# A fused four-layer kernel, first phase: group-level VectorE work dealt out over more units, half of the gathers placed one unit sooner, sorted rows loaded in six transfers

## The chip, the cores and the metric

One core of one Trainium2 chip. The metric is the device time of one execution in microseconds, the median over several runs. The engines are PE (TensorE), DVE (VectorE), ACT (ScalarE), POOL (GpSimd) and SP (SyncE, which here only issues DMAs). A line number such as L741 is a line of the kernel before.

## The reference, cut to what matters

Four layers, each a cross attention and a feed-forward part with a residual; batch 32, 128 rows, width 128, all float32. The first phase of the kernel computes layer 0 and the attention of layer 1:

```python
x = x + L0_xattn(layernorm(x), ctx, ctx, mask0, wo, bo)      # 16 heads of 8, softmax, relu(ctx @ wo.T + wo_b)
x = x + L0_ffn(layernorm(x), Wr, br, W1, b1, W2, b2)         # 8 experts, top 2, hidden 512
x = x + L1_xattn(layernorm(x), ctx, ctx, mask1, ...)         # 16 heads of 8, softmax
# L0_ffn, for each row: logits = x @ Wr + br; the two largest, softmax of them as gates;
# out = sum over the two experts e of gate[e] * (relu(x @ W1[e] + b1[e]) @ W2[e] + b2[e])
```

Every expert is applied only to the rows that chose it: the rows are sorted by expert in DRAM, and gathered back afterwards.

## The kernel before, in words

The batch is cut into 8 groups of 4 batch entries (512 rows). The first phase runs 16 streams one after another: stream j = 0 to 7 is the attention of layer 0 for group j, stream 8 to 15 the attention of layer 1 for group j - 8. Each stream has 8 units (u = 0 to 7, 8 heads of one batch entry each), so there are 128 units, n = 8 j + u, and 16 more steps for what trails. In unit n PE computes scores (L851), DVE adds or clips with the mask (L582, L586) and reduces to the negative row maximum (L1206), ACT applies the exponential (L981); one unit later PE transposes the result (L865) and ACT and DVE copy it out (L973, L976 or L1213), two units later PE multiplies by the values (L883), then turns the result back (L890), and DVE normalises it (L1184, L1188). Each engine runs its own instructions in order; a function work(place, n) of each engine holds what is done once per group, hung on a unit and a place in it. DVE has places 0 to 3; place 3 is the end of its unit, behind the maximum.

Work done once per group, and where it stands before the change (stream j runs, u is the unit in it):

- front: LayerNorm of the next layer 0 stream's rows. DVE statistics at u = 0, place 3 (L1091 and L1092; the instructions are L329, L333, L336), the power on POOL at u = 1 (L340), the scaling on DVE at u = 1 (L345), transposes on PE at u = 3 (L730), copy qT on ACT (L929), queries on DVE at u = 4 (L1057).
- router of the group two streams back: comparisons on DVE at u = 0, place 3 (router_dve), gates at u = 2, place 3 (router_gates_dve), turned by PE at u = 4 (L810) and copied by DVE at u = 4 (L1159).
- ranking, once for each pair of groups, at u = 2, place 3: rank_dve gives the sorted place of each row (the index, last line L436), rank_tiles_dve the expert of each of 23 tiles (L443 to L447), rank_gates_dve the two gates of each row (L456 to L460).
- scatter: POOL writes the rows to sorted_in in DRAM by 16 indirect DMAs, four per unit at u = 4 to 7 (L1035).
- load: SP reads all 23 sorted tiles (128 rows of 128) back to SBUF, one unit before the pair's first tile unit (load_sorted, L689). It waits for the scatters and, from the second pair on, for the turns of the pair before.
- tiles: four pairs of groups, their tiles in units 34 to 50, 51 to 67, 68 to 84 and 85 to 101. For each pair there are 6 turns (PE transposes a quad of 4 tiles, L741; ACT copies, L904), 23 hidden products (L747; relu on ACT L911 or DVE L1067), 23 output products (L755), 6 copies back (L919) and stores to sorted_out (L709). The first tile unit has turn 0 and three hidden tiles; the second turn stands in the next unit, the later ones three units apart. SP loads the weights of a tile four tiles ahead (L682); it waits for the output product that frees the buffer.
- gathers: for layer 1's stream of group g POOL gathers 4 + 4 blocks of rows from sorted_out at the start of u = 0 of the stream before (L1011), and DVE adds them with their gates (combine, L1076 and L1081) at u = 3, place 3, just ahead of the late statistics (L1112; L329 again). Then follow power (L340), scaling at u = 4 (L345), transposes (L730), query product.
- last_ln: DVE statistics at u = 7, place 3, power on POOL at u = 7.

PE's bank 6 serves all of this group-level work in turn; each use waits until the use before has been read (function aux).

## Time and profile before

| what | value |
|---|---|
| median of 3 runs | 2143.19 us (2140.99 to 2145.85) |
| the profiled execution's own time | 2141.56 us |
| its span | 2139.8 us |
| mean granted TensorE clock | 0.955 |
| busy over the span: PE, DVE, ACT, POOL | 87%, 70%, 61%, 29% |
| first phase, from unit 0's maximum to the last unit's | 45.4 to 839.1 us |

The span is from the first to the last instruction of one profiled execution. The granted clock is the share of full TensorE speed that the chip allowed. In a row of the trace in order of time the first number is the start in us from the span's start, the second the duration in us, then engine, line, operation, what is written <- what is read, shape and count; in brackets the idle time of the engine just before it and what ended that.

### The profile page before, as it was taken

What the parts mean: (1) busy time and instruction counts of PE and PEld (TensorE: products, weight loads), DVE (VectorE), ACT (ScalarE), POOL (GpSimd) and SP (SyncE); (2) the same over time, 40 slices, a digit from 0 to 9 for tenths busy, and PEclk for the clock granted to TensorE, in tenths of its full rate; (3) what the DMA queues carried; (4) which work ended last, traced back from release to release, by engine and by line L of the source; (5) the groups of instructions that cost most, each with busy time, mean ns of one, the idle gap of its engine ahead of it and who ended that gap; (6) DMA issues with size and microseconds to landing.
All of it is one profiled execution on the core that took longest, in us unless ns stands there. A gap on an engine that the chain in (4) does not pass through costs nothing.

```text
span 2139.8 us, 49953 instructions
## 1 busy us (share of the span) xinstructions
PE 1861.7 (87%) x17669; PEld 1515.4 (71%) x17669; DVE 1488.4 (70%) x3873; ACT 1303.8 (61%) x4466; POOL 617.2 (29%) x610
## 2 busy tenths in 40 slices
PE   3987998989989988657888889999999988898878
PEld 2776887778878776545666677777877876676665
DVE  5887786878878887666776675766757565655556
ACT  1976665556666777536676766666666654544432
POOL 0003031131522220024343333254452523333321
PEclk9998999999999999858899989999999999999999
DMA  8013354354544100310000011222222223232351
GB/s 242 17 31 102 108 151 141 118 163 128 156 146 144 50 21 6 130 46 20 29 6 15 6 43 38 87 81 85 73 73 69 82 82 95 72 99 72 109 146 49
DMA packets 119637, 178.44 MB, mean 83 GB/s; under 512 B 9824, under 2 KB 77728, under 8 KB 119136
## 3 DMA queue, kind: packets, MB, share of 16 engines
q1 hardware_dynamic: 111712, 159.51, 24.6%
q0 software_dynamic: 7680, 15.74, 2.4%
q8 instruction: 144, 2.36, 0.5%
q14 instruction: 101, 0.83, 0.1%
HBM read 141.26 MB, written 33.95 MB: 82 GB/s over the span
## 4 chain that ended last, share of the span: by engine, by line
PE 37%; DVE 9%; ACT 6%; issue 4%; POOL 1%; DMA 0%; DVEq 0%; ACTq 0%; SPq 0%
PE ps L1659 5%; PE ps L1944 5%; PE ps L1892 3%; PE ps L1697 3%; PE ps L1885 3%; ACT pb L2093 3%; PE ps L1681 2%; PE ps L1866 2%; PE ps L1688 2%; PE ps L1670 2%; DVE nm L2472 2%; PE ps L1707 1%; PE ps L1715 1%; PE ps L1914 1%; PE ps L1858 1%
## 5 line engine op out<-in xcount | busy, mean ns | idle before, releaser
L2093 ACT ACTIVATE pb<-ps,nm 128x128 f32<-128x128 f32 x1024 | 364.1, 379 | 196.0 <-DVE nm L2472 195.9
L2141 POOL TENSOR_TENSOR pb<-pb,rcs 128x512 f32<-128x512 f32 x256 | 268.5, 1050 | 663.0 <-DVE rcs L2480 662.2
L981 ACT ACTIVATE pb<-pb,nm 128x128 f32<-128x128 f32 x1024 | 313.2, 394 | 31.7 <-DVE nm L1206 29.9
L2497 DVE COPY pt<-ps 128x512 f32<-128x512 f32 x128 | 88.3, 690 | 198.2 <-PE ps L1944 198.1
L2093 ACT ACTIVATION_READ_ACCUMULATOR pb<-ps,nm 128x1 f32 x1024 | 222.5, 217 | 0.0
L2472 DVE TENSOR_REDUCE nm<-ps 128x8 f32<-128x1024 f32 x128 | 155.9, 1218 | 63.5 <-PE ps L1892 40.3
L1944 PE MATMUL ps<-w,pb 128*128 128x128 f32 x1024 | 167.4, 288 | 22.5 <-ACT pt L2101 10.3
L1206 DVE TENSOR_REDUCE nm<-pb 128x8 f32<-128x1024 f32 x128 | 156.2, 1220 | 4.4
L1944 PEld LDWEIGHTS ps<-w,pb 128*128 128x128 f32 x1024 | 121.4, 147 | 46.6 <-ACT pt L2101 20.1
L865 PE MATMUL ps<-w,pb 128*128 128x128 f32 x1024 | 145.9, 287 | 5.4 <-ACT pb L981 5.2
L2101 ACT ACTIVATE pt<-ps 128x512 f32<-128x512 f32 x128 | 77.0, 602 | 91.0 <-PE ps L1944 90.9
L865 PEld LDWEIGHTS ps<-w,pb 128*128 128x128 f32 x1024 | 125.1, 149 | 9.7 <-issue 7.5
L1659 PE MATMUL ps<-hT,big 128*128 128x128 f32 x840 | 116.8, 283 | 13.8 <-DVE hT L2243 13.4
L1659 PEld LDWEIGHTS ps<-hT,big 128*128 128x128 f32 x840 | 105.0, 194 | 33.5 <-DVE hT L2243 21.0
L973 ACT ACTIVATE pt<-ps 128x512 f32<-128x512 f32 x128 | 76.4, 597 | 65.5 <-PE ps L865 64.4
L747 PE MATMUL ps<-h_all,big 128*128 128x128 f32 x736 | 104.3, 287 | 12.2 <-DVE hT L1067 5.7
L747 PEld LDWEIGHTS ps<-h_all,big 128*128 128x128 f32 x736 | 93.3, 198 | 19.0 <-DVE hT L1067 7.5
L966 ACT ACTIVATE ou<-ps 128x256 f32<-128x256 f32 x128 | 48.4, 378 | 92.9 <-DVE h_all L1188 47.0
L755 PE MATMUL ps<-big,hT 128*128 128x128 f32 x736 | 101.7, 282 | 0.0
L1975 ACT ACTIVATE hT<-ps 128x256 f32<-128x256 f32 x133 | 50.9, 383 | 75.7 <-PE ps L1659 75.0
L755 PEld LDWEIGHTS ps<-big,hT 128*128 128x128 f32 x736 | 92.1, 196 | 5.5 <-issue 2.2
L1681 PE MATMUL ps<-h_all,big 128*128 128x512 f32 x128 | 71.5, 640 | 26.3 <-ACT h_all L2014 26.3
(379 smaller groups left out, 4407.0 us busy)
## 6 DMA issues: line engine op xcount, KB each, us to landing
big<-in_we SPq DMA_DIRECT2D x92, 514.0 KB, 3.7
big<-in_we SPq DMA_DIRECT2D x109, 384.0 KB, 3.1
sorted_out<-big SPq DMA_DIRECT2D x27, 256.0 KB
big<-sorted_in SPq DMA_DIRECT2D x7, 960.0 KB, 5.7
sorted_in<-big SPq DMA_DIRECT2D x4, 1472.0 KB, 12.2
hidden<-h_all SPq DMA_DIRECT2D x7, 512.0 KB, 2.9
h_all<-hidden SPq DMA_DIRECT2D x7, 512.0 KB, 3.8
sorted_out<-h_all SPq DMA_DIRECT2D x14, 256.0 KB
```

What stands on the lines that cost most here:

```text
L747: m = pe.matmul(ps[:, 5, c * P:(c + 1) * P], w1_0[:, k % NWS, c, :], xsT0[:, (NQ0 * g + t // 4) % 4, (t % 4) * P:(t % 4 + 1) * P], start=T ...
L755: m = pe.matmul(ps[:, 7, (t % 4) * D:(t % 4 + 1) * D], hT[:, k % 4, c * P:(c + 1) * P], w2_0[:, k % NWS, c, :], start=(c == 0), stop=(c == ...
L865: m = pe.transpose(ps[:, 2 + k // 4, (k % 4) * S:(k % 4 + 1) * S], pb[:, p % 2, k * S:(k + 1) * S], ident)
L981: m = a.activation(pb[:, n % 2, k * S:(k + 1) * S], pb[:, n % 2, k * S:(k + 1) * S], ACT.Exp, bias=nm[:, n % 2, k:k + 1])
L1206: v.tensor_reduce(nm[:, n % 2, :], buf, AX, ALU.max, negate=True).then_inc(s["maxed"], 1)
L1659: m = pe.matmul(ps[:, bank, (2 * half + c) * P:(2 * half + c + 1) * P], weights[:, half, c, :], rows_T, start=True, stop=True)
L1681: pe.matmul(ps[:, BANK_A, :], q3_w[:, c, :], yT3[g % 2], start=True, stop=True)\
L1944: m = pe.transpose(ps[:, BANK_T, k * S:(k + 1) * S], pb[:, p % 2, (4 * half + k) * S:(4 * half + k + 1) * S], ident)
L2093: m = a.activation(pb[:, n % 2, e * S:(e + 1) * S], ps[:, score_bank(n) + half, k * S:(k + 1) * S], ACT.Exp, bias=nm[:, n % 2, e:e + 1], a ...
L2141: g_.tensor_tensor(p4, p4, r4.unsqueeze(2).to_broadcast([P, 4, S]), ALU.mult).then_inc(n2["p_normed"], 1)
L2472: v.tensor_reduce(nm[:, n % 2, :], ps[:, bank:bank + 2, :].rearrange("p a (j k) -> p (a j) k", k=S), AX, ALU.max, negate=True).then_inc(n2 ...
L2497: v.tensor_copy(pt[:, p % 2, 4 * S:8 * S], ps[:, BANK_T, :]).then_inc(n2["p_lo"], 1)
```

## The change

- The front statistics move from u = 0 to u = 7, place 3, of the unit before; those of group 1 stay in unit 0.
- combine moves from u = 3 to u = 2, place 3; the late statistics stay.
- rank_tiles_dve and rank_gates_dve move from u = 2 to u = 3, place 3.
- Of the eight gathers of a group the first four, with their waits, stand at the end of u = 7 in POOL's program, the other four where all stood.
- load_sorted issues six transfers, one per quad. Transfers 3 to 5 wait until the transfer three places before has landed; three semaphores take turns. A turn waits for its own quad.
- The semaphore group_loaded, which nothing used, goes.

```diff
--- before.py
+++ after.py
@@ -247,7 +247,6 @@
             counted.append(s)
             return s
 
-        group_loaded = isem("group_loaded")
         loaded = [isem(f"loaded_{n}") for n in range(2)]
         v_pool = isem("v_pool")
         v_dve = isem("v_dve")
@@ -301,6 +300,7 @@
                                                    "row_psum", "row_added", "down_read", "q2_psum", "q2_col", "v2_psum",
                                                    "bias_bo2", "bias_bos", "bias_bout3"]))
         weights_loaded = [isem(f"weights_loaded_{n}") for n in range(NWS)]
+        sorted_quads = [isem(f"sorted_quad_{q}") for q in range(3)]
         moe = {name: isem(f"moe_{name}") for name in
                ["sel", "rank", "index", "tiles", "scattered", "gathered", "sorted_loaded", "xT_psum", "xT", "turned_back",
                 "stored", "first_added", "b2_added", "logits", "logit_row", "shifted", "gate_exp", "gates", "gateT_psum", "gateT", "hid_psum",
@@ -684,10 +684,15 @@
 
                 def load_sorted(g):
                     sp.wait_ge(moe["scattered"], 16 * 2 * PB * (g + 1))
-                    if g:
-                        sp.wait_ge(moe["xT_psum"], NQ0 * g)
-                    sp.dma_start(xs0[:, :, :], xs_d[g].rearrange("(t p) d -> p t d", p=P))\
-                        .then_inc(moe["sorted_loaded"], 16)
+                    for q in range(NQ0):
+                        first, end = quad(q, NT0)
+                        if g:
+                            sp.wait_ge(moe["xT_psum"], NQ0 * (g - 1) + q + 1)
+                        if q >= 3:
+                            sp.wait_ge(sorted_quads[q % 3], 16 * (2 * g + 1))
+                        sp.dma_start(xs0[:, first:end, :],
+                                     xs_d[g].rearrange("(t p) d -> p t d", p=P)[:, first:end, :])\
+                            .then_inc(sorted_quads[q % 3], 16)
 
                 loads(0)
                 for n in range(NUN):
@@ -736,7 +741,7 @@
                         pe.wait_ge(*before0[(g, kind, t)])
                     if kind == "turn":
                         first, end = quad(t, NT0)
-                        pe.wait_ge(moe["sorted_loaded"], 16 * (g + 1))
+                        pe.wait_ge(sorted_quads[t % 3], 16 * (2 * g + t // 3 + 1))
                         for i in range(first, end):
                             m = pe.transpose(ps[:, 5, (i - first) * P:(i - first + 1) * P], xs0[:, i, :], ident)
                         m.then_inc(moe["xT_psum"], 1)
@@ -996,21 +1001,20 @@
                     g_.tensor_copy(vas[j % 2][:, :, :, 0:DH].rearrange("p b h d -> p (b h) d"),
                                    ctx[:, :, :].rearrange("p b (h d) -> p (b h) d", h=H)).then_inc(v_pool, 1)
 
+                def gather(g, ks):
+                    for k in ks:
+                        e = k // G * PB + g % 2 * G + k % G
+                        g_.indirect_dma_start(yg0[:, k, :], None, ys_d[g // 2],
+                                              bass.IndirectOffsetOnAxis(ap=sort0[g // 2].idx[:, e:e + 1], axis=0))\
+                            .then_inc(moe["gathered"], 16)
+
                 pow_(front, 1)
                 values(0, 0)
                 for n in range(NUN + 2 * NU):
                     j, u = divmod(n, NU)
                     layer, g = stream(j + 1)
                     if layer == 1 and u == 0:
-                        g_.wait_ge(moe["stored"], 16 * NQ0 * (g // 2 + 1))
-                        if g:
-                            g_.wait_ge(moe["gathered"], 16 * 2 * G * g)
-                            g_.wait_ge(moe["combined"], g)
-                        for k in range(2 * G):
-                            e = k // G * PB + g % 2 * G + k % G
-                            g_.indirect_dma_start(yg0[:, k, :], None, ys_d[g // 2],
-                                                  bass.IndirectOffsetOnAxis(ap=sort0[g // 2].idx[:, e:e + 1], axis=0))\
-                                .then_inc(moe["gathered"], 16)
+                        gather(g, range(G, 2 * G))
                     if layer == 0 and u == 1:
                         pow_(front, g + 1)
                     if layer == 0 and u == 2:
@@ -1034,6 +1038,13 @@
                         for k in range(4 * (u - 4), 4 * (u - 3)):
                             g_.indirect_dma_start(xs_d[p], bass.IndirectOffsetOnAxis(ap=sort0[p].idx[:, k:k + 1], axis=0),
                                                   expert_ys[(2 * p + k % PB // G) % 3][:, k % G, :], None).then_inc(moe["scattered"], 16)
+                    layer, g = stream(j + 2)
+                    if layer == 1 and u == 7:
+                        g_.wait_ge(moe["stored"], 16 * NQ0 * (g // 2 + 1))
+                        if g:
+                            g_.wait_ge(moe["gathered"], 16 * 2 * G * g)
+                            g_.wait_ge(moe["combined"], g)
+                        gather(g, range(G))
                 g_.wait_ge(moe["gathered"], 16 * 2 * G * NG)
                 g_.wait_ge(moe["scattered"], 16 * 2 * G * NG)
 
@@ -1088,8 +1099,10 @@
                     j, u = divmod(n, NU)
                     here = (place, u)
                     layer, g = stream(j + 1)
-                    if layer == 0 and here == (3, 0):
-                        stats(front, g, g + 1)
+                    if n == 0 and place == 3:
+                        stats(front, 1, 2)
+                    if stream(j + 2)[0] == 0 and here == (3, 7):
+                        stats(front, g + 1, g + 2)
                     if layer == 0 and here == (3, 1):
                         v.wait_ge(front.yT_psum, g)
                         apply(front, g, g + 1)
@@ -1107,8 +1120,9 @@
                                         ps[:, 6, :].rearrange("p (b h d) -> p b h d", b=G, h=H),
                                         R("bv1").rearrange("p (h d) -> p h d", h=H).unsqueeze(1)
                                         .to_broadcast([P, G, H, DH]), ALU.add).then_inc(v_dve, 1)
+                    if layer == 1 and here == (3, 2):
+                        combine(g)
                     if layer == 1 and here == (3, 3):
-                        combine(g)
                         stats(late, g, g + 1)
                     if layer == 1 and here == (3, 4):
                         v.wait_ge(late.yT_psum, g)
@@ -1152,8 +1166,9 @@
                         router_gates_dve(v, link, picked0[g % 2], gates0[g % 2], g + 1)
                         if g % 2:
                             rank_dve(v, link, sort0[g // 2], sel_z[:, 0:PB, :], 6, g // 2 + 1)
-                            rank_tiles_dve(v, link, sort0[g // 2])
-                            rank_gates_dve(v, link, sort0[g // 2], gates[:, :, :])
+                    if layer == 0 and g % 2 and here == (3, 3):
+                        rank_tiles_dve(v, link, sort0[g // 2])
+                        rank_gates_dve(v, link, sort0[g // 2], gates[:, :, :])
                     if layer == 0 and here == (1, 4):
                         v.wait_ge(moe["gateT_psum"], g + 1)
                         v.tensor_copy(gateT, ps[0:E0, 6, :]).then_inc(moe["gateT"], 1)
```

## Rows read from the trace of the kernel before

**Rows 1.** Stretch 33.5 to 845 us: busy PE, PEld, DVE, ACT, POOL; PEclk, DMA, GB/s.
```profile
33.50:845.00 811.50, 727.50 (x7884) 622.02 (x7884) 647.31 (x1547) 553.54 (x1634) 173.13 (x175) 0.96 0.34 101
```

**Rows 2.** Waits of PE, 100 to 845 us: total us, times, longest.
```profile
PE ps L741 <- DMA big<-sorted_in: 18.5, 4, 6.8
...
PE ps L810 <- ACT qT L929: 6.2, 4, 2.9
```

**Rows 3.** PE in order of time: the four waiting turns, and transposes behind one.
```profile
215.19 1.12 PE L741 MATMUL ps<-w,big 128*128 128x128 f32 x4 [6.75 <-DMA big<-sorted_in]
...
337.54 1.09 PE L741 MATMUL ps<-w,big 128*128 128x128 f32 x4 [3.98 <-DMA big<-sorted_in]
338.42 1.92 PE L865 MATMUL ps<-w,pb 128*128 128x128 f32 x8
...
349.16 1.04 PE L865 MATMUL ps<-w,pb 128*128 128x128 f32 x8
...
468.45 1.09 PE L741 MATMUL ps<-w,big 128*128 128x128 f32 x4 [4.46 <-DMA big<-sorted_in]
...
599.83 1.09 PE L741 MATMUL ps<-w,big 128*128 128x128 f32 x4 [3.31 <-DMA big<-sorted_in]
```

**Rows 4.** SP's queue in order of time, around the loads of pairs 0 and 1.
```profile
207.32 0.72 SPq L689 DMA_DIRECT2D big<-sorted_in  x1
...
328.64 0.74 SPq L689 DMA_DIRECT2D big<-sorted_in  x1
330.17 3.60 SPq L682 DMA_DIRECT2D big<-in_we  x1
```

**Rows 5.** Issue to landing in us: L689 (1472 KB), L682 (514 KB), 960 KB loads.
```profile
DMA to landing us min/median/max: 7.8/9.3/10.4
...
DMA to landing us min/median/max: 3.3/3.7/9.4
...
big<-sorted_in SPq DMA_DIRECT2D x7, 960.0 KB, 5.7
```

**Rows 6.** DVE, then PE, in order of time, around unit 16.
```profile
109.82 0.21 DVE L1184 RECIPROCAL rc<-ps 128x8 f32<-128x8 f32 x1 [0.87 <-PE ps L890]
...
113.37 0.86 DVE L329 BATCH_NORM_STATS2 st_front<-x_all 128x6 f32<-128x128 f32 x4
...
114.76 0.18 DVE L356 TENSOR_TENSOR lg<-ps,rows 128x32 f32<-128x32 f32 x1
...
118.56 0.62 PE L883 MATMUL ps<-pt,h_all 128*9 128x128 f32 x16 [1.40 <-ACT ou L966]
```

**Rows 7.** DVE, then PE, in order of time, units 26 to 28.
```profile
168.56 0.16 DVE L443 TENSOR_TENSOR cmp_a<-cmp_a 128x8 f32<-128x8 f32 x1
...
170.72 0.21 DVE L1184 RECIPROCAL rc<-ps 128x8 f32<-128x8 f32 x1
...
176.67 1.01 PE L810 MATMUL ps<-w,gates 128*8 128x128 f32 x4 [2.88 <-ACT qT L929]
```

**Rows 8.** POOL in order of time: pair 0's last scatter, group 6's last gather.
```profile
204.76 0.96 POOL L1035 DMA_INDIRECT sorted_in<-hT,big  x1 [0.30 <-issue]
...
740.43 0.95 POOL L1011 DMA_INDIRECT big<-sorted_out,big  x1 [0.30 <-issue]
```

**Rows 9.** DVE in order of time, unit 68.
```profile
468.28 0.67 DVE L1159 COPY big<-ps 8x512 f32<-8x512 f32 x1
```

**Rows 10.** PE at 652 and 710 us, DVE in units 106 and 107, in order of time.
```profile
652.45 0.66 PE L741 MATMUL ps<-w,big 128*128 128x128 f32 x4 [0.84 <-DVE hT L1067]
...
710.55 1.08 PE L730 MATMUL ps<-w,y 128*128 128x128 f32 x4 [1.59 <-DVE y L345]
...
738.92 1.22 DVE L1206 TENSOR_REDUCE nm<-pb 128x8 f32<-128x1024 f32 x1
...
744.56 1.13 DVE L1076 SCALAR_TENSOR_TENSOR x_all<-big,x_all 128x128 f32<-128x128 f32 x4
...
746.90 0.87 DVE L329 BATCH_NORM_STATS2 st_late<-x_all 128x6 f32<-128x128 f32 x4
```

## The prediction

> **What bounds the kernel now.** I read four views, in this order. First the busy time of the stretch that the change touches: the 128 units of the first phase. PE is busy 727.5 of 811.5 us there, DVE 647.3, ACT 553.5, at a mean granted clock of 0.96 [rows 1]. So PE leads and DVE is close behind; what can be won is PE's 84 us of waits and its time at the lower clock. I count units from 0 by the row-maximum reductions (L1206). Second, the waits of PE. The largest group, 18.5 us in four waits, is the turn of the sorted rows (L741) waiting for the load from sorted_in [rows 2]. Third, PE in order of time: the four waits are 6.75, 3.98, 4.46 and 3.31 us, at 215, 338, 468 and 600 us [rows 3], one for each pair of groups, in units 33/34, 51, 68 and 85. The reader should also see what follows such a wait: the eight transposes of L865 take 1.92 us, and 1.04 us a unit later [rows 3]. That is one half and full clock (1.2 and 2.4 GHz). Fourth, DVE around its heavy units, to see whether its bursts reach PE; they do in some (below).
>
> **Sorted rows in six transfers.** Now one load of 1472 KB lands 7.8, 9.3 or 10.4 us (least, median, most) after its issue [rows 5], and the first turn waits for all of it although it reads four of 23 tiles, 256 KB. No row has a 256 KB part of it. From below: 960 KB of the same pattern land in 5.7 us [rows 5], so (7.8 - 5.7) / 512 KB is 0.0041 us per KB, and 256 KB come to 5.7 - 704 x 0.0041 = 2.8 us, an estimate. From above: a 514 KB weight load, 3.7 us median and 9.4 at worst [rows 5]. I take 3.5, near the first two, and keep 9.4 for a rival.
> - Pair 0: issued at 207.32 [rows 4], first quad at 210.8 instead of the turn at 215.19: 4.4 us.
> - Pair 1: issued at 328.64 [rows 4], quad at 332.1. PE was ready at 337.54 - 3.98 = 333.56, so all 3.98 go.
> - Pair 2: landing within 10.4 us of issue means issue at 458 or later, quad by 461.6 or little after; PE was ready at 463.99. But the next use of the auxiliary bank, L786, waits for DVE's copy L1159, and DVE is in an unbroken row of work until that copy ends at 468.28 + 0.67 = 468.95 [rows 9]. The turn and L865 took 2.6 us from 468.45 to L786 at 471.0. So only 471.0 - 468.95 = 2.1 us go, the rest becomes a wait for DVE.
> - Pair 3: PE was ready at 599.83 - 3.31 = 596.5; all 3.3 go.
> - Clock: behind pair 1's wait L865 costs 1.92 - 1.04 = 0.9 us too much [rows 3]; the turn ahead of it (half as many matmuls) and the eight matmuls behind it run at the same clock, by the same ratio 0.4 and 0.8: 2.1 us. Of this I take half at pairs 1 and 3, 2.1 in all, since smaller waits stay.
>
> Together 4.4 + 4.0 + 2.1 + 3.3 + 2.1 = **15.9 us**. On SP's queue the five more issues (some 0.4 us each) and the waits of transfers four to six for the landing of one to three stand ahead of the next weight load and of the store of a finished quad. The sixth can be issued about 3.5 + 2 = 5.5 us after the first. That costs nothing as long as this queue is no more blocked than now: the weight load behind the big transfer already sits 3.6 us and more in its issue [rows 4], so that SP is free only at about 334.5, 5.9 us after 328.64. The third hidden tile needs that weight some 8 us later. The later quads are read one to four units (7 us each) later. Cost taken: 0.
>
> The Trainium skill (DMA: Bandwidth & Descriptors, section "Anatomy of one DMA — SWDGE (gpsimd) path") fits a transfer by 2.0 us plus bytes over 436 GB/s, which speaks against splitting: six times 2.0 us fixed instead of once. By it the first quad would land in 2.6 us and the whole load in 5.5; the trace disagrees on the latter, 7.8 at least [rows 5]. With the page's value the pair 0 term would be 5.3 instead of 4.4.
>
> **LayerNorm statistics of the front stream one unit sooner.** They take 114.76 - 113.37 = 1.4 us of DVE [rows 6] and now share the unit with the router's comparisons. In unit 16 this makes PE wait 1.40 us for the context (L883) behind ACT behind DVE [rows 6]. In the unit before, DVE waits 0.87 us before its reciprocal [rows 6] and again before the mask, so the 1.4 us find room. Gain 1.4 in unit 16 and 1.4 in 24, the same pattern. Unit 32 gains nothing: there all waits for pair 0's scatters on POOL, which run back to back to 204.76 + 0.96 [rows 8]. Units 8, 40 and 48: 0.3 in all, since PE is nearly without wait there. **3.1 us.**
>
> **Tile table and gates of the ranking one unit later.** 170.72 - 168.56 = 2.2 us of DVE [rows 7], four times. In unit 26 they delay the maximum, so the exponentials, so ACT's copy of qT, for which PE's L810 waits 2.88 us [rows 7]. I take 1.7 of the 2.2. Pair 1 has the same wait inside the total of 6.2 us in four [rows 2]; less is left there because expert matmuls fill PE: 1.0. In pairs 2 and 3 the combine moves the other way between the same two units, so DVE's sum is unchanged: 0. **2.7 us.** SP's first weight loads wait for this table; it comes no later in time than it is needed, as they are used 8 units on.
>
> **Gathers.** POOL's order does not change. The four gathers that now stand at the end of unit u = 7 are directly followed by the other four at the start of u = 0, with nothing between them, and the waits ahead of them are the same. Gain and cost 0; queued behind them is only POOL's next power.
>
> **Combine one unit sooner.** 746.90 - 744.56 = 2.3 us of DVE [rows 10] leave the unit of the late statistics. Groups 0 to 3: 0. Group 4: PE's wait of 0.84 us for the hidden tile [rows 10] goes: 0.8. Group 5: the wait of 1.59 us for y goes (L730) [rows 10], and with it 0.9 of the 2 us that the low clock costs behind such a wait. Against it: combine now needs its gathers one unit sooner, and the gathers don't come sooner. The landing time is not in the trace; the nearest row is the scatter's, 207.32 - 205.72 = 1.6 us from the end of its last issue to SP's load [rows 4, 8]. Group 6: the last gather ends its issue at 741.38 [rows 8], lands at 743.0; DVE reaches the combine at 738.92 + 1.22 = 740.1 [rows 10] and waits 2.9 us. It ends at 745.3; normalising and mask 1.6, maximum 1.1, bias 0.6 follow, so the late statistics start at 748.7 instead of 746.90 [rows 10]: 1.8 us later. Group 7, the same with 1.1 us less wait: 0.8. Sum 0.8 + 1.6 + 0.9 - 2.6 = **0.7 us**.
>
> **Sum.** 15.9 + 3.1 + 2.7 + 0.7 = 22.4 us. The profiled execution took 2141.56 us (span 2139.8), 1.6 us under the median of the runs, 2143.19; the gain is taken off either. From the median: 2120.8 us.
>
> **Rivals.**
> - *More than the sum.* The clock comes back wholly after all stalls (2 us more), the bursts of DVE behind L883, L810 and L730 vanish earlier, the first quad lands in 2.8 us and the gathers before DVE asks: some 10 us more, 2111. For it: DVE has no wait in most heavy units. Against: moved work is not removed.
> - *First quad late.* It shares the engines with weight loads that need up to 9.4 us [rows 5]; at 9 us the four waits stay, and only 6.5 us are won: 2136.7.
> - *SP blocked.* If a quad takes 5 us, transfer six goes out after 11 us and the weight for the third hidden tile comes 3 to 4 us late, at three pairs: 10 us back, 2131. For it: its issue is already blocked 3.6 us [rows 4]. Against: the blockage is part of today's time too.
> - *Slower: DVE waits for gathers.* The combine stands in order on DVE, ahead of the next mask and maximum. With gathers that land x us later than 1.6, groups 6 and 7 lose x each, groups 3 to 5 too beyond about 3 us of slack. That reaches the other 25 us at x about 7, a landing of 8 to 9 us; beyond, at 10, the kernel takes 2147. Only the large load shows such landings [rows 5], and a gather moves 64 KB.
> - *Not what it says.* The gathers' part, certain by the order on POOL; it is in the sum.
>
> **Chances.** Forecast (gain 15 to 28) 0.62; more 0.12; first quad late 0.11; SP blocked 0.09; slower 0.04; a trade that leaves nothing 0.02. The range takes the first four, 2111 to 2134. A change under 0.2%, 4.3 us, cannot be told from none in this kernel. Faster by more 0.91, within 0.05, slower 0.04.
>
> **What would show it.** L741 waits for sorted_in under 3 us in sum, only at pair 0; transfers about 3.5 us to landing; units 16 and 24 about 1.4 us shorter; L810 waits under 1 us at unit 28; eight gathers still 1.27 us apart in one row; a new wait of DVE at the first combine line near units 106 and 114. Wrong if L741 still waits 3 us and more at pairs 1 to 3, if L747 waits for weights behind the quads, or if DVE's wait for gathers shows in groups 3 to 5.

## The result and the profile after

The changed kernel takes 2115.11 us (median of 4 runs, 2109.54 to 2117.64), the kernel before 2144.52 in the runs timed with it (2140.99 to 2152.38). The ratio is 0.9863, 95% interval 0.9838 to 0.9888: 1.4% faster. The forecast, 2120.8 us or a ratio of 0.9896, was right in its direction and its range (2111 to 2134), and too small in its size: the gain between the two medians is 29.4 us, 22.4 were forecast, and 29.4 lies a little above the band of 15 to 28 that the prediction gave to its forecast, in that of the rival "more than the sum". The profiled execution took 2117.64 us with a span of 2115.9, 23.9 us under that of before.

The code is longer, so behind the sorted load the line numbers of the changed kernel are 4 to 15 higher, save those of the gathers: L741, L747, L786 and L865 became L746, L752, L791 and L870; L883 became L888 and L810 L815; L1076 and L1206 became L1087 and L1221; the gathers are L1007, the sorted load L693.

First the stretch of the 128 units, which answers to [rows 1] (busy PE, PEld, DVE, ACT, POOL; granted clock, DMA share, GB/s):

```profile
33.50:819.50 786.00, 721.78 (x7884) 615.33 (x7884) 646.60 (x1546) 553.15 (x1634) 172.91 (x175) 0.97 0.35 104
```

The stretch is 25.5 us shorter with the same 7884 matmuls. DVE does as much as before (646.6 us against 647.3); PE's busy time fell by 6 us, as fewer of its matmuls ran at half clock (granted 0.97 instead of 0.96); the other 20 us are waits of PE that are gone. Next the waits of PE in this stretch, the view of [rows 2] (total us, times, longest):

```profile
PE ps L791 <- DVE big L1174: 7.3, 4, 3.0
PE ps L752 <- DMA big<-in_we: 6.9, 4, 2.6
...
PE ps L815 <- ACT qT L934: 3.9, 3, 1.6
PE ps L888 <- ACT ou L971: 3.8, 4, 2.1
PE ps L746 <- DMA big<-sorted_in: 2.6, 1, 2.6
```

The wait of the turns for the sorted rows was 18.5 us in four and is 2.6 in one, at pair 0. A new one stands in its place: the hidden products wait 6.9 us for weights. In the kernel before these stood at 1.9 us, and the waits for the context (L883, now L888) at 8.9:

```profile
PE ps L883 <- ACT ou L966: 8.9, 10, 1.5
...
PE ps L747 <- DMA big<-in_we: 1.9, 2, 1.1
```

PE in order of time shows where (compare [rows 3]):

```profile
202.25 1.12 PE L746 MATMUL ps<-w,big 128*128 128x128 f32 x4 [2.64 <-DMA big<-sorted_in]
...
318.16 1.16 PE L856 MATMUL ps<-ctxT,qm 32*128 32x128 f32 x16
...
326.94 2.05 PE L752 MATMUL ps<-h_all,big 128*128 128x128 f32 x8 [2.25 <-DMA big<-in_we]
328.92 2.08 PE L856 MATMUL ps<-ctxT,qm 32*128 32x128 f32 x16
...
450.46 1.09 PE L791 MATMUL ps<-w,h_all 128*128 128x128 f32 x4 [2.82 <-DVE big L1174]
...
581.18 1.13 PE L752 MATMUL ps<-h_all,big 128*128 128x128 f32 x8 [2.59 <-DMA big<-in_we]
582.24 1.78 PE L856 MATMUL ps<-ctxT,qm 32*128 32x128 f32 x16
```

These are pair 0, the third hidden tile of pairs 1 and 3, and at pair 2 the wait for DVE's copy that the prediction named. Behind the weight waits PE runs at half clock again: the sixteen matmuls of L856 took 1.16 us ahead of the wait and take 2.08 and 1.78 behind it. SP's queue at pair 1 answers to [rows 4]:

```profile
314.54 6.46 SPq L693 DMA_DIRECT2D big<-sorted_in  x6
321.77 1.47 SPq L682 DMA_DIRECT2D big<-in_we  x2
```

The six issues hold SP for 6.5 us, and the next weight load leaves 7.2 us after the first of them. The times from issue to landing of the 24 transfers (20 of 256 KB, four of 192 KB), which answer to [rows 5]:

```profile
DMA to landing us min/median/max: 2.8/3.5/5.7
```

Last, DVE in order of time in units 106 and 107, the view of [rows 10]:

```profile
711.00 1.22 DVE L1221 TENSOR_REDUCE nm<-pb 128x8 f32<-128x1024 f32 x1
715.02 1.14 DVE L1087 SCALAR_TENSOR_TENSOR x_all<-big,x_all 128x128 f32<-128x128 f32 x4 [2.80 <-DMA big<-sorted_out,big]
...
720.73 0.86 DVE L329 BATCH_NORM_STATS2 st_late<-x_all 128x6 f32<-128x128 f32 x4
```

Combine waits 2.80 us for its gathers; at group 7 it waits 1.85. It waits at group 3 too, in unit 82, 0.45 us:

```profile
559.51 1.14 DVE L1087 SCALAR_TENSOR_TENSOR x_all<-big,x_all 128x128 f32<-128x128 f32 x4 [0.45 <-DMA big<-sorted_out,big]
```

### The profile page after: what moved, and what is told of

The parts are those of the page before. It is cut to its first block, busy times and chain, and to the rows that moved or that the text cites. A ratio compares the mean times of both kernels' runs of the same rounds, so it can differ in the third digit from the quotient of the medians.

```text
span 2115.9 us, 49981 instructions
## 1 busy us (share of the span) xinstructions
PE 1859.6 (88%) x17665; PEld 1511.9 (71%) x17669; DVE 1486.2 (70%) x3873; ACT 1302.6 (62%) x4466; POOL 616.5 (29%) x610
## 4 chain that ended last, share of the span: by engine, by line
PE 38%; DVE 9%; ACT 6%; issue 4%; POOL 1%; DMA 0%; DVEq 0%; ACTq 0%; SPq 0%
PE ps L1674 5%; PE ps L1959 5%; PE ps L1907 3%; PE ps L1712 3%; PE ps L1900 3%; ACT pb L2108 3%; PE ps L1696 3%; PE ps L1881 2%; PE ps L1703 2%; PE ps L1685 2%; PE ps L1722 1%; DVE nm L2487 1%; PE ps L1730 1%; PE ps L1929 1%; PE ps L1873 1%
## 5 line engine op out<-in xcount | busy, mean ns | idle before, releaser
L1221 DVE TENSOR_REDUCE nm<-pb 128x8 f32<-128x1024 f32 x128 | 156.2, 1220 | 4.4
L870 PE MATMUL ps<-w,pb 128*128 128x128 f32 x1024 | 141.8, 280 | 8.2 <-ACT pb L986 7.9
L870 PEld LDWEIGHTS ps<-w,pb 128*128 128x128 f32 x1024 | 120.4, 146 | 13.6 <-issue 10.6
L752 PE MATMUL ps<-h_all,big 128*128 128x128 f32 x736 | 103.9, 286 | 12.2 <-DMA big<-in_we 6.9
L752 PEld LDWEIGHTS ps<-h_all,big 128*128 128x128 f32 x736 | 92.9, 198 | 18.6 <-issue 9.1
```

The lines of the kernel that those rows point to most:

```text
L752: m = pe.matmul(ps[:, 5, c * P:(c + 1) * P], w1_0[:, k % NWS, c, :], xsT0[:, (NQ0 * g + t // 4) % 4, (t % 4) * P:(t % 4 + 1) * P], start=T ...
L870: m = pe.transpose(ps[:, 2 + k // 4, (k % 4) * S:(k % 4 + 1) * S], pb[:, p % 2, k * S:(k + 1) * S], ident)
L1221: v.tensor_reduce(nm[:, n % 2, :], buf, AX, ALU.max, negate=True).then_inc(s["maxed"], 1)
```

## The experiments

All edits concern the first phase, so I read each profile by one marker, the start of the last unit's maximum (839.1 us before, 813.5 changed), and by the lengths of short stretches of units, measured between starts of the maximum. A table of the lengths follows the last experiment. The experiments ran in three sessions, each on another chip. Six transfers alone, all but the six transfers and both repairs ran five or six times and have a ratio; each other kernel ran once, so of it only the profile is read, and no ratio is claimed.

**Six transfers alone.** Edit, to the kernel before (the unused group_loaded goes too):

```diff
-                    sp.dma_start(xs0[:, :, :], xs_d[g].rearrange("(t p) d -> p t d", p=P))\
-                        .then_inc(moe["sorted_loaded"], 16)
+                    for q in range(NQ0):
...
+                        if q >= 3:
+                            sp.wait_ge(sorted_quads[q % 3], 16 * (2 * g + 1))
+                        sp.dma_start(xs0[:, first:end, :],
+                                     xs_d[g].rearrange("(t p) d -> p t d", p=P)[:, first:end, :])\
+                            .then_inc(sorted_quads[q % 3], 16)
```

> The kernel before, with the sorted rows loaded in six transfers as the only edit (the unused semaphore group_loaded makes room for the new ones). Marker: the start of the last unit's maximum, 839.1 us before, 813.5 with the whole change. Theory 1, the sum of the prediction: the six transfers carry 15.9 us, so the marker is at 823 and the kernel takes 0.9926 of before. Theory 2, SP blocked: the issue of six transfers holds SP for 6 to 7 us, the third hidden tile of pairs 1 and 3 waits for its weights, 2 to 3 us each and the clock falls again, so only 11 to 12 us are left: marker at 827 to 828, ratio 0.995. In both the wait of the first turn for sorted_in stays only at pair 0, at 2 to 3 us. Theory 3, the waits were only covering DVE's backlog: under 6 us.

Ratio 0.9931 (0.9897 to 0.9965), which takes in both theories; marker 828.15, as theory 2 has it. Counted from unit 9 on, past units 0 to 8, which took 1.6 us longer here than before, 13.1 us were won: more than the 11 to 12 of theory 2, less than 15.9. The waits are those of theory 2, 2.28 us at pair 1 and 2.02 at pair 3. All waits of PE for DMAs in this kernel:

```profile
PE ps L752 <- DMA big<-in_we: 6.2, 4, 2.3
...
PE ps L746 <- DMA big<-sorted_in: 2.1, 1, 2.1
```

The weight waits at the third hidden tile are there with the six transfers alone, so they come from these. Units 85 and 86 together took 18.97 us, 21.90 before: of the 3.3 us wait and its clock, 2.9 us were won.

**All but the six transfers.** The same edit taken out of the changed kernel.

> The whole change without the six transfers (one load of 1472 KB again). Theory 1, the terms of the prediction for everything else: 3.1 + 2.7 + 0.7 = 6.5 us, marker at 832.6 (839.1 before), ratio 0.997. Theory 2, the steps read unit by unit from the changed kernel: units 16 and 24 1.3 each, units 26 to 28 4.2, units 90 to 101 about 4, units 106 and 114 minus 2.4: some 10 us, marker at 829. Theory 3, the parts need each other (the DVE work only matters once the load no longer stalls PE): under 3 us. If parts add up, the gains of this run and of the run with the six transfers alone give 25.6 together.

Ratio 0.9930 (0.9907 to 0.9954), marker 826.43, where the terms of the prediction gave 832.6. Counted from unit 9 to 127 the two halves won 13.1 and 12.5 us, 25.7 with rounding; the whole change won 25.1 in its first profile and 28.9 in another (below). So they add up as far as two profiles can tell, and theory 3 falls. The half without the transfers carried twice what I gave it (6.5). It won this although PE's waits for the one big load grew, from 18.5 us to 23.0: PE arrives earlier at a load that does not.

**A semaphore for each transfer.** In the changed kernel:

```diff
+        sorted_quads += [slot["hid_psum"], slot["hid"], slot["logits"]]
...
-                        if q >= 3:
-                            sp.wait_ge(sorted_quads[q % 3], 16 * (2 * g + 1))
...
-                            .then_inc(sorted_quads[q % 3], 16)
+                            .then_inc(sorted_quads[q], 16)
...
-                        pe.wait_ge(sorted_quads[t % 3], 16 * (2 * g + t // 3 + 1))
+                        pe.wait_ge(sorted_quads[t], 16 * (g + 1))
```

The three further semaphores are ones of the kernel's last phase; they are cleared between the phases.

> The changed kernel, each of the six transfers with a semaphore of its own, so that transfers four to six do not wait for the landing of one to three. Theory 1 (SP is held by these waits, and the new waits of L752 for weights, 2.25 us at pair 1 and 2.59 at pair 3, come from that): the six issues take 2.5 to 3 us instead of 6.5 to 7.1, the waits for weights at the third hidden tile vanish, the marker moves from 813.5 to 807 to 811. Theory 2 (the queue takes no more descriptors, as when the weight load sat 3.6 us in its issue behind the single load): the time moves into a long issue of transfer four to six or of the weight load, the waits stay, marker 813 to 814.

Marker 806.05. The weight waits at the third hidden tile are gone, but the six issues did not shrink to 3 us where other DMAs stood ahead. SP's queue of this kernel, pairs 0 and 1 (its code is two lines longer, so the weight loads are L684):

```profile
200.45 3.12 SPq L693 DMA_DIRECT2D big<-sorted_in  x6
...
315.07 5.33 SPq L693 DMA_DIRECT2D big<-sorted_in  x6
321.15 1.48 SPq L684 DMA_DIRECT2D big<-in_we  x2
```

And PE in order of time, the third hidden tile of pair 1:

```profile
326.46 1.16 PE L752 MATMUL ps<-h_all,big 128*128 128x128 f32 x8 [1.23 <-ACT hT L916]
```

Both theories are partly right. At pair 0 the issues take 3.1 us. At pair 1 they still take 5.3, one of them 1.87 us by itself: SP sits in the issues themselves, with no wait in the program. With both repairs (below) the same six took 4.0. The weight load leaves 6.1 us after the first transfer instead of 7.2. That 1.1 us is enough for the weights to arrive before ACT has emptied the bank, and the clock stays up: unit 51 takes 9.16 us at a granted clock of 1.00 instead of 11.68 at 0.76, units 85 and 86 16.59 at 1.00 instead of 20.73 at 0.84. One profile would be thin evidence, since the weight wait at pair 1 varies without any edit near it: over the eight profiles with six transfers and three semaphores it is 1.45 to 2.60 us, and in the two where it is shortest (gathers at u = 6 with 1.45, front statistics back with 1.51) unit 51 takes 9.35 and 9.41 us at full clock. But it is there in all eight, at pair 3 in seven of the eight, and at neither pair in the two profiles with six semaphores.

**Gathers really sooner.** In the changed kernel both halves of the gathers go to u = 6, ahead of the power of last_ln:

```diff
-                    if layer == 1 and u == 0:
-                        gather(g, range(G, 2 * G))
...
+                    layer, g = stream(j + 2)
+                    if layer == 1 and u == 6:
+                        g_.wait_ge(moe["stored"], 16 * NQ0 * (g // 2 + 1))
...
+                        gather(g, range(2 * G))
                     layer, g = stream(j - 1)
                     if layer is not None and u == (7 if layer else 5):
                         pow_(last_ln if layer else experts, g + 1)
...
-                    if layer == 1 and u == 7:
...
-                        gather(g, range(G))
```

> The changed kernel with all eight gathers and their waits one unit and a half sooner in POOL's program: at u = 6, ahead of the power of last_ln at u = 7. Theory 1 (the gathers start late because they stand behind POOL's wait for the last_ln statistics, and combine waits for them): combine's waits for sorted_out, 2.80, 1.85 and 0.45 us, vanish, and the marker moves 3 to 5 us, to 809 to 810.5. Theory 2 (the landing is late because of the DMA, not the order): the waits stay, marker at 813.5. Theory 3: POOL waits for the stores and holds up the power behind them, new waits of DVE for rs_last_ln, marker no better.

Marker 801.15, 12.4 us ahead of 813.5 where 3 to 5 were expected. Not all of that is the gathers': unit 51 and units 66 to 69 are 2.3 and 2.1 us shorter too, and 66 to 69 are as short in an unedited second profile (below). What the edit gave stands past unit 106: from there to the last unit's maximum 94.86 us, 102.51 and 99.52 in the two profiles of the changed kernel, 100.13 before, so 4.7 to 7.7 us. No wait of combine is left. POOL in order of time shows group 6's last gather ahead of the power, and in the changed kernel behind it the first, at 702.48:

```profile
696.73 0.95 POOL L1007 DMA_INDIRECT big<-sorted_out,big  x1 [0.30 <-issue]
697.70 1.05 POOL L340 TENSOR_TENSOR rs_last_ln<-ve_last_ln,half 128x4 f32<-128x4 f32 x1
```

```profile
701.28 1.02 POOL L340 TENSOR_TENSOR rs_last_ln<-ve_last_ln,half 128x4 f32<-128x4 f32 x1 [15.70 <-DVE ve_last_ln L336]
702.48 1.01 POOL L1007 DMA_INDIRECT big<-sorted_out,big  x1 [0.19 <-issue]
```

Units 106 to 109 take 17.68 us; 21.76 in the changed kernel, 20.13 before. In this profile the 2.80 us of waiting thus cost 4.1 us. Behind that wait of DVE, PE in the changed kernel waited too and fell to half clock:

```profile
718.37 0.62 PE L888 MATMUL ps<-pt,h_all 128*9 128x128 f32 x16 [2.13 <-ACT ou L971]
...
722.82 1.92 PE L870 MATMUL ps<-w,pb 128*128 128x128 f32 x8
```

It need not. In the second profile of the changed kernel DVE waits 2.73 us and PE 2.06 at the same places, and the clock stays up:

```profile
717.89 0.62 PE L888 MATMUL ps<-pt,h_all 128*9 128x128 f32 x16 [2.06 <-ACT ou L971]
...
718.82 1.16 PE L856 MATMUL ps<-kT,h_all 32*128 32x128 f32 x16
```

The stretch of units 106 to 109 as the windows show it (the clock is the last number but two), first profile, then second:

```profile
711.00:732.80 21.80, 19.66 (x201) 15.71 (x202) 16.48 (x39) 15.33 (x45) 4.20 (x4) 0.84 0.04 11
```

```profile
710.60:731.10 20.50, 17.00 (x200) 13.29 (x201) 16.27 (x39) 15.27 (x45) 4.22 (x4) 1.00 0.04 11
```

There the wait costs 2.8 us, 20.50 against 17.68: its own length and no more.

**Both repairs.** The two edits above together.

> The changed kernel with both edits that moved the marker: six semaphores for the six transfers, and all eight gathers at u = 6. Marker 813.5 with the change, 806.1 with the semaphores, 801.2 with the gathers. If the two act on different waits (weights at the third hidden tile; gathers at combine), they add up: marker at 793.7 to 795, ratio to before near 0.979. If both only shorten the same reserve of PE, under 3 us more than the gathers alone: marker above 798.

2100.75 us (2093.40 to 2107.45, 5 runs), ratio 0.9815 (0.9790 to 0.9840), marker 797.56. It is faster than the kernel before. By the two ratios to before it is some 0.5% under the changed one, but their intervals just overlap (up to 0.9840 and from 0.9838), so against the changed kernel the profile must carry the rest; against the gathers alone (one run, 2096.93 us) the times say nothing. In it unit 51 (9.16 us), units 85 and 86 (16.59) and units 106 to 109 (17.67) are each as short as in the better of the two single repairs, so the repairs act on different waits. The two single repairs put the marker 7.5 and 12.4 us ahead of 813.5, which would give 793.7 together. It is 4 us later, between the two answers expected (793.7 to 795; above 798). The single marker of the gathers held 2.3 us of unit 51, which the semaphores give too, and 2.1 of units 66 to 69, where one profile happened to keep the full clock; markers of one kernel differ by 3.4 us (below).

**Gathers together.** The gathers' part of the change undone: all eight at the start of u = 0.

> The changed kernel with the gathers' part undone: all eight gathers with their waits at the start of u = 0, as before the change. Theory 1 (the program order of POOL is the same, since nothing stands between the end of u = 7 and the start of u = 0): marker within 0.5 us of 813.5, gathers 1.27 us apart, the same waits of combine, 2.8, 1.9 and 0.5 us. Theory 2 (half of the gathers really start sooner in the changed kernel): combine waits longer by a unit, some 4 us at each of two groups, marker 818 and more.

Marker 810.83, combine waits 2.89, 1.64 and 0.67 us. Theory 1: this part of the change does nothing. The marker is even 2.7 us lower, outside the 0.5 us expected, though POOL's order is the same, and that had to be explained before any part could be read by its marker.

**The changed kernel once more.** No edit.

> The changed kernel itself, once more. If the profiles repeat apart from chance shifts, the marker lies between 810 and 815, combine waits 2.8, 1.9 and 0.5 us for its gathers, L752 waits about 2 us each for weights at pairs 1 and 3, and the first turn of pair 0 waits 2.6 us. If the marker comes out under 809 or over 817, the single-profile comparisons of the parts below 4 us say nothing by their marker.

Marker 810.12, span 2105.8. Combine waits 2.73, 1.74 and 0.77 us, L752 2.18 and 2.39 at pairs 1 and 3, the first turn 2.78, all close to what was expected. So the same kernel gives 813.5 and 810.1, and spans 10 us apart; the four timed runs of the changed kernel alone spread from 2107.8 to 2115.9 in span. The stretches in the table show that most repeat within 0.1 us and a few have two or more lengths, 1 to 2 us apart. Where they differ by more than 0.3 us, the granted clock differs. First and second profile: unit 20 takes 6.21 us at 1.00 and 7.86 at 0.78; units 26 to 28 17.54 at 0.90 and 16.78 at 1.00; 58 to 60 24.91 at 1.00 and 26.35 at 0.94; 66 to 69 35.34 at 0.90 and 33.22 at 1.00; 74 to 76 24.64 at 0.93 and 23.25 at 1.00; 106 to 109 21.76 at 0.84 and 20.50 at 1.00. Parts are read by stretches from here on. Behind the phase the time varies too: 1302.4 us from the marker to the end in one profile, 1295.7 in the other, 1300.7 before, 1294.0 to 1305.9 over all kernels here, none of which is edited there.

**Combine back at u = 3.**

```diff
-                    if layer == 1 and here == (3, 2):
-                        combine(g)
                     if layer == 1 and here == (3, 3):
+                        combine(g)
                         stats(late, g, g + 1)
```

> The changed kernel with combine back at u = 3 of every group. By the prediction's term the marker moves 0.7 us later, to 814.2. By the steps read unit by unit (units 82 to 84 gained 1.5, 90 to 92 1.5, 98 to 101 2.4; units 106 and 114 lost 1.6 and 0.8) it moves 3.0 us later, to 816.5. Rival: with the tile table now at u = 3 too, the burst of DVE in units 59 and 75 grows to 2.3 + 2.2 + 1.4 us at one place and PE waits more there: 818 and more. The waits of combine for gathers vanish in any case.

Marker 817.39. Units 82 to 84, 90 to 92 and 98 to 101 are back at 18.77, 19.57 and 26.05 us, the values of before; units 106 to 109 and 114 to 119 at 20.13 and 32.30, those of before too (21.76 and 33.05 in the first profile of the changed kernel, 20.50 and 31.33 in the second). And the rival shows at pair 2: units 58 to 60 take 28.73 us, more than ever, since combine, statistics and the tile table now stand in one place, and PE waits for the copy behind them:

```profile
393.94 1.09 PE L791 MATMUL ps<-w,o 128*128 128x128 f32 x4 [5.23 <-DVE big L1173]
```

In the changed kernel, second profile, the same wait is 2.99 us. So the two moves need each other at pair 2; alone, the move of the tile table would have cost some 2.3 us there (28.73 against 26.46 before), by this one profile.

**Tile table and gates back at u = 2.**

```diff
-                    if layer == 0 and g % 2 and here == (3, 3):
-                        rank_tiles_dve(v, link, sort0[g // 2])
-                        rank_gates_dve(v, link, sort0[g // 2], gates[:, :, :])
...
                             rank_dve(v, link, sort0[g // 2], sel_z[:, 0:PB, :], 6, g // 2 + 1)
+                            rank_tiles_dve(v, link, sort0[g // 2])
+                            rank_gates_dve(v, link, sort0[g // 2], gates[:, :, :])
```

> The changed kernel with the tile table and the gates of the ranking back at u = 2. By the prediction's term the marker moves 2.7 us later, to 816.2. By the steps of units 26 to 29 (4.2 us) and 42 to 45 (1.0 us) it moves 5.2 us later, to 818.7, with L815 waiting 2.9 us again at unit 28. Rival: at pairs 2 and 3 combine and the whole ranking then stand in one unit, 2.3 us more in a burst than ever before: another 2 us or more, marker above 820.5.

Marker 817.40. Units 26 to 28 take 19.86 us at a clock of 0.91, 2.3 more than the first profile with the move (0.90) and 3.1 more than the second (1.00), and L815 waits 2.9 us again; units 42 to 44 take 0.3 more, where I had 1.0. The rival at pairs 2 and 3 shows little: 27.03 us at pair 2 against 26.35 in the second profile (the first had 24.91, at full clock), and nothing at pair 3.

**Front statistics back at u = 0.**

```diff
-                    if n == 0 and place == 3:
-                        stats(front, 1, 2)
-                    if stream(j + 2)[0] == 0 and here == (3, 7):
-                        stats(front, g + 1, g + 2)
+                    if layer == 0 and here == (3, 0):
+                        stats(front, g, g + 1)
```

> The changed kernel with the front statistics back at u = 0. By the prediction's term the last maximum is 3.1 us later, by the steps at units 16 and 24 (1.3 us each) 2.6 us. Marker 813.5 in the first profile of the changed kernel and 810.8 in the one that differed from it only in where the gathers stand in the text; so single markers differ by 2 to 3 us, and the unit pairs count: units 15 and 16 together 11.46 us as before the change (10.14 with it), units 23 and 24 the same. Rival: once the load no longer stalls PE the statistics matter in the tile period too, units 39 and 40 and 47 and 48 over 1 us longer each.

Marker 819.61. Units 15 and 16 take 11.45 us again, 23 and 24 too. The rival holds as well: units 39 and 40 take 14.06 against 12.67, units 47 and 48 15.28 against 14.18. The surprise is at units 26 to 28: 24.36 us, 6.8 to 7.6 more than with the statistics moved and 2.6 more than before the change. The reason is the clock: 0.64 over these three units, 0.81 before the change, 0.90 and 1.00 in the two profiles of the changed kernel. Busy time of the engines in this kernel, in three stretches (the clock is the last number but two):

```profile
150.00:160.00 10.00, 8.60 (x105) 7.43 (x105) 9.43 (x26) 6.75 (x21) 1.62 (x2) 0.99 0.10 28
160.00:176.00 16.00, 16.00 (x101) 14.33 (x103) 10.62 (x33) 6.89 (x21) 4.08 (x4) 0.50 0.04 13
176.00:177.50 1.50, 1.50 (x21) 0.81 (x22) 0.55 (x4) 1.44 (x5) 0.00 (x0) 0.70 0.13 44
```

PE in order of time inside the second stretch, the transposes and the ranking's products:

```profile
162.84 1.91 PE L870 MATMUL ps<-w,pb 128*128 128x128 f32 x8
...
164.88 3.51 PE L410 MATMUL ps<-sel_z,ones 128*128 128x64 f32 x16
```

The kernel before went through the same place like this:

```profile
160.00:165.00 5.00, 5.00 (x39) 4.88 (x37) 4.83 (x13) 3.94 (x12) 0.00 (x0) 0.66 0.00 0
165.00:173.00 8.00, 6.85 (x89) 5.66 (x90) 6.07 (x24) 3.66 (x11) 3.13 (x3) 1.00 0.17 42
```

In both, the front statistics of unit 24 make PE wait 1.4 us, and a few us later the clock is at half. Before, it is back by 165 us; here it stays for 16 us in which PE is never idle. What keeps it there is not shown. With the statistics moved the wait is not there; in the second profile of the changed kernel the clock is at 1.00 from 150 to 185 us:

```profile
150.00:185.00 35.00, 32.09 (x388) 27.00 (x386) 32.25 (x81) 26.63 (x77) 7.48 (x8) 1.00 0.23 79
```

The lengths of the stretches, in us, all from starts of the maximum:

| units | before | changed | once more | six alone | all but six | own semaphores | gathers u = 6 | combine back | tables back | front back |
|---|---|---|---|---|---|---|---|---|---|---|
| 15, 16 | 11.46 | 10.14 | 10.14 | 11.46 | 10.14 | 10.14 | 10.15 | 10.14 | 10.14 | 11.45 |
| 26 to 28 | 21.75 | 17.54 | 16.78 | 21.62 | 17.63 | 16.77 | 16.78 | 17.56 | 19.86 | 24.36 |
| 34 | 16.23 | 11.24 | 11.36 | 11.76 | 15.77 | 11.24 | 11.39 | 11.28 | 11.31 | 11.35 |
| 47, 48 | 15.28 | 14.19 | 14.18 | 15.28 | 14.18 | 14.18 | 14.19 | 14.17 | 14.18 | 15.28 |
| 51 | 15.24 | 11.68 | 10.97 | 10.97 | 15.96 | 9.16 | 9.35 | 10.82 | 12.02 | 9.41 |
| 58 to 60 | 26.46 | 24.91 | 26.35 | 26.38 | 26.40 | 26.54 | 26.55 | 28.73 | 27.03 | 26.52 |
| 66 to 69 | 37.47 | 35.34 | 33.22 | 34.99 | 37.54 | 34.18 | 33.20 | 34.47 | 33.20 | 34.17 |
| 85, 86 | 21.90 | 20.73 | 20.94 | 18.97 | 23.83 | 16.59 | 20.05 | 18.22 | 21.26 | 20.63 |
| 90 to 92 | 19.57 | 18.03 | 18.02 | 19.56 | 18.02 | 18.02 | 18.02 | 19.57 | 18.02 | 18.02 |
| 98 to 101 | 26.06 | 23.62 | 23.62 | 24.42 | 23.62 | 23.62 | 23.62 | 26.05 | 23.63 | 23.63 |
| 106 to 109 | 20.13 | 21.76 | 20.50 | 20.48 | 20.64 | 21.75 | 17.68 | 20.13 | 20.61 | 21.80 |
| 106 to 126 | 100.13 | 102.51 | 99.52 | 98.83 | 99.76 | 100.78 | 94.86 | 100.13 | 99.79 | 100.85 |
| 9 to 126 | 757.33 | 732.22 | 728.46 | 744.19 | 744.80 | 724.45 | 719.44 | 735.64 | 735.46 | 737.88 |

## Why the prediction was right

The direction and the mechanism of each large term came as forecast. One cost was missed, the other terms together came to twice their forecast, and that the sum still came near is in part luck.

- **Sorted rows in six transfers, 15.9 us: the mechanism held, one cost was missed.** The turns wait for sorted rows only at pair 0, 2.6 us. The 3.5 us that I took is the median of all 24 transfers; the first quads, which alone end the wait, landed in 2.8, 4.2, 4.2 and 5.0 us at pairs 0 to 3. That cost nothing, though at pair 3 the quad landed only 0.2 us before its turn. The transfers alone won 4.5 us in unit 34, 4.3 in unit 51, 2.5 in units 66 to 69 and 2.9 in units 85 and 86, against 4.4, 5.1, 2.1 and 4.4 forecast with their share of the clock; in the changed kernel the wait for DVE's copy at pair 2 stands where it was forecast, 2.82 us. Over units 9 to 126 they won 13.1 of the 15.9. The step that failed is "Cost taken: 0" for SP's queue. It compared 5.5 us for the sixth issue with the 5.9 us of today; at pair 1 the sixth issue came 6.0 us and the weight load 7.2 us after the first transfer. I also gave the third hidden tile some 8 us of slack beyond SP's release, and forgot that PE now arrives earlier. At pair 1 PE wanted this tile 10.2 us after the issue of the first transfer, 15.8 before the change, and the weights arrived 5.2 us after their own issue. With six semaphores unit 51 and units 85 and 86 are 2.5 and 4.1 us shorter than in the changed kernel, so the missed cost was up to 6 to 7 us. The "SP blocked" rival was thus partly true: the right place, at two pairs instead of three, and less than its 10 us.
- **Front statistics, 3.1 us: right per unit (1.3 at units 16 and 24, 1.4 forecast), too small in sum.** Units 39 and 40 gave 1.4 more, of which unit 41 took back 0.7; units 47 and 48 gave 1.1, which unit 49 took back. And the half clock that follows the wait at unit 24 runs into the ranking. Unit 32 gained 1.3 and unit 33 gave 1.1 of it back, where DVE now waits 0.8 us for POOL's power behind pair 0's scatters: the prediction had taken 0 there for this reason.
- **Tile table, 2.7 us: 2.3 to 3.1 at units 26 to 28 by taking it back, 1.7 forecast;** at pair 1 0.3 instead of 1.0. Together with the statistics these units won 4.2 to 5.0 us, part of it clock (granted 0.81 before, 0.90 and 1.00 after); this is the largest part of the surplus. L815 still waits 1.62 us at unit 28, where I had said under 1.
- **Combine, 0.7 us: the gain was too small, the loss right in its waits and not steady in its cost.** Forecast 0.8 us at group 4 and 2.5 at group 5; 1.5 and 2.4 measured. Group 3, taken at 0, gave 1.4 in spite of its own wait of 0.45 us. Group 6 waited 2.80 us (forecast 2.9) and lost 1.6 (1.8) in one profile, 0.4 in the other; group 7 waited 1.85 (1.8) and lost 0.8 (0.8) in one; in the other units 114 to 119 are 1.0 us shorter than before, the clock at 1.00 instead of 0.95. The landing time of a gather, taken from the scatters as 1.6 us, held: the last issue ends at 713.45, combine goes on at 715.02.
- **Gathers, 0: right.** The order on POOL didn't change, and undoing the part changed nothing that two profiles of one kernel don't differ by.
- **The sum, 22.4 us:** 25.1 and 28.9 in the stretch of units 9 to 126, 29.4 in the medians, with an interval from 24 to 35. The two halves, each by itself, show the errors: the transfers won 13.1 us where 15.9 were forecast, 2.8 too little, and the rest 12.5 where 6.5 were forecast, 6.0 too much. Two errors of opposite sign met in the sum.

Of the prediction's own signs of being wrong two appeared: the hidden products wait for weights behind the quads, and DVE waits for gathers at group 3 (0.45 and 0.77 us). The first is the missed cost; the second stayed small. And the range of the prediction, 2111 to 2134, was said to take in the rival "first quad late", whose own time, 2136.7, lies outside it. In its rival on the gathers it said that only the large load lands in 8 to 9 us, though its own rows have a weight load at 9.4.

The rival "more than the sum" was in part true as well: PE's waits for ACT behind bursts of DVE, at L888 and L815, did shrink (8.9 to 3.8 us, 6.2 to 3.9, each counted to 6 us past the last unit's maximum).

## What to carry to other kernels

When a change makes an engine arrive earlier, check every transfer behind the moved one against the new arrival, not the old: slack shrinks by what is gained. An instruction that is written sooner in an in-order program goes out sooner only if something stood between its old place and its new one; here a wait for another engine just ahead of both places kept the gathers where they were. And read the granted clock beside a wait of the matrix engine: about the same wait (2.80 and 2.73 us of DVE, 2.13 and 2.06 of PE) cost 4.1 us where the clock then fell and 2.8 where it did not, in two profiles of one kernel.

## What the runs showed of the hardware that was not expected

The clock can stay at half for 16 us while PE is never idle (front statistics back, 160 to 176 us), and in the kernel before be back within 5 us at the same place (160 to 165 us). The wait ahead of it was 1.4 us in both. And behind a wait of 2.1 us it can fall or not in the same kernel (0.84 and 1.00 over units 106 to 109 of the changed one). What decides this was not tried.

An issue on SP's queue can be held up even when nothing in the program waits: six transfers of 512-byte rows held it 3.1 us at pair 0, and at pair 1, where a weight load had been issued 0.4 us before, 5.3 us with one issue of 1.87 us, or 4.0 us in the kernel with both repairs. Whether it is the rows, the bytes or the load ahead that holds them was not tried.

Two profiles of one kernel differ by 10 us in span (2115.9 and 2105.8), 3.4 of it in the first phase, and there mainly in a few stretches with several lengths, which go with the granted clock. A part of 2 us is told by its stretch, to 0.1 us where the clock is the same, and not by the total.
